# Ending of a fused projection and stream-mixing kernel re-ordered by tile, and its first loads put on one queue

## The reference, cut to what matters

```
h = einsum('bsi,boi->bso', x, weight[ids])          # 8 batches, 512 x 2048 by 2048 x 2048
hn = h * rsqrt(mean(h*h) + eps)
res, pre, post = hn@W_res.T+b, hn@W_pre.T+b, hn@W_post.T+b     # 16, 4 and 4 logits a token
H_res = (1-g)*I + g*sinkhorn(res, 50 iterations, tau 0.1)
pre, post = softmax(pre), softmax(post)
streams = h.reshape(B, T, 4, 512)
y = einsum('btnc,btn->btc', streams, pre) @ W_branch
out = x + einsum('btij,btjc->btic', H_res, streams) + einsum('btc,btn->btnc', y, post)
```

## Time and profile before

| | |
|---|---|
| median of 3 runs | 1717.91 us (1715.99 to 1718.01) |
| the profiled execution's own time | 1717.58 us |
| its span | 1715.8 us |
| PE busy | 1686.2 us (98%) |
| DVE busy | 1425.7 us (83%) |
| ACT busy | 719.8 us (42%) |
| DMA | 252.41 MB, mean 147 GB/s |

### The profile page before, as it was taken

The page is one execution under the profiler, slowest core; times in us unless marked ns, Lnnn a source line. Parts: engine busy times, 40 slices in busy tenths (PEclk is TensorE's granted clock), DMA queues, the critical chain, the costliest instruction groups (busy, mean ns, idle before and its releaser), DMA issues.

```text
span 1715.8 us, 24502 instructions
## 1 busy us (share of the span) xinstructions
PE 1686.2 (98%) x7740; PEld 1363.0 (79%) x7740; DVE 1425.7 (83%) x5973; ACT 719.8 (42%) x1167; POOL 101.5 (6%) x142
## 2 busy tenths in 40 slices
PE   8999999999999999999999999999999999999886
PEld 7888888888888878887888888888788887888773
DVE  4322499988998889988899979998899889998795
ACT  4433544244333343434433354424433454334563
POOL 0000000010000100000000000001000110001021
PEclk9999999999999999999999999999999999999999
DMA  6223423375233832358325562337522693238779
GB/s 238 87 92 125 152 87 111 99 216 189 99 109 113 253 140 98 103 151 264 99 90 128 186 212 98 111 102 218 187 96 87 168 317 101 89 97 217 175 136 247
DMA packets 68865, 252.41 MB, mean 147 GB/s; under 512 B 7936, under 2 KB 8064, under 8 KB 67840
## 3 DMA queue, kind: packets, MB, share of 16 engines
q1 hardware_dynamic: 48576, 177.97, 31.6%
q0 software_dynamic: 19584, 71.31, 17.5%
q10 hardware_dynamic: 576, 1.57, 0.3%
HBM read 203.63 MB, written 42.99 MB: 144 GB/s over the span
## 4 chain that ended last, share of the span: by engine, by line
PE 89%; issue 4%; DMA 3%; DVE 3%; POOL 1%; ACT 1%; SPq 0%; DVEq 0%; POOLq 0%; ACTq 0%
PE acc L1169 77%; PE y_ps L1247 3%; PE turn_ps L1205 3%; PE logit_ps L1213 2%; PE logit_ps L1216 2%; DVE piece L1027 2%; DMA x_raw<-xn 1%; DMA piece<-xn 1%; DMA out<-late_own 1%; DVE w_lo L778 1%; PE acc L1356 1%; PE y_ps L1237 1%; POOL out L427 1%; PE acc L1194 0%; PE turn_ps L1225 0%
## 5 line engine op out<-in xcount | busy, mean ns | idle before, releaser
L1169 PE MATMUL acc<-w_hi,x_hi 128*128 128x512 f32 x2040 | 807.7, 396 | 0.0
L1169 PE MATMUL acc<-w_hi,x_lo 128*128 128x512 f32 x2040 | 796.0, 390 | 0.0
L1169 PE MATMUL acc<-w_lo,x_hi 128*128 128x512 f32 x2040 | 794.4, 389 | 0.0
L473 ACT ACTIVATE w_hi<-w_raw 128x1024 fp32r<-128x1024 f32 x255 | 269.3, 1058 | 441.6 <-DMA w_raw<-wt 441.5
L1169 PEld LDWEIGHTS acc<-w_hi,x_lo 128*128 128x128 f32 x2040 | 382.9, 188 | 82.3
L1169 PEld LDWEIGHTS acc<-w_hi,x_hi 128*128 128x128 f32 x2040 | 383.2, 188 | 79.6
L1169 PEld LDWEIGHTS acc<-w_lo,x_hi 128*128 128x128 f32 x2040 | 383.6, 188 | 76.7
L778 DVE TENSOR_TENSOR w_lo<-w_raw,w_hi 128x1024 fp32r<-128x1024 f32 x256 | 311.7, 1218 | 133.8 <-ACT w_hi L473 122.4
L1027 DVE SCALAR_TENSOR_TENSOR piece<-cond,kern,piece 128x512 f32<-128x512 f32 x416 | 283.1, 746 | 5.0 <-DMA piece<-xn 5.0
L963 DVE RECIPROCAL vec<-vec 128x8 f32<-128x8 f32 x1536 | 240.4, 198 | 0.0
L961 DVE TENSOR_REDUCE vec<-work 128x8 f32<-128x32 f32 x1536 | 238.0, 194 | 0.2
(11 more groups left out here) (161 smaller groups left out, 835.7 us busy)
## 6 DMA issues: line engine op xcount, KB each, us to landing
w_raw<-wt SPq DMA_DIRECT2D x255, 512.0 KB, 3.5
out<-piece POOLq DMA_DIRECT2D x62, 512.0 KB, 5.4
x_raw<-xt SPq DMA_DIRECT2D x61, 512.0 KB, 5.4
piece<-xn POOLq DMA_DIRECT2D x56, 512.0 KB, 7.1
out<-late_own POOLq DMA_DIRECT2D x10, 512.0 KB, 9.0
grouped<-cond SPq DMA_DIRECT2D x16, 256.0 KB, 9.4
x_raw<-xn POOLq DMA_DIRECT2D x8, 512.0 KB, 12.0
out<-x_raw SPq DMA_DIRECT2D x7, 512.0 KB, 10.9
```

The costliest lines, as they stand in the source:

```text
L473: nc.scalar.activation(w_hi[:, unit % HI_SLOTS, :, :], w_raw[:, unit % LO_SLOTS, :, :], ACT.Copy).then_inc(w_hi_ready, 1)
L1169: mm = nc.tensor.matmul(acc[t][:], stationary, moving, start=(chunk == 0 and m == 0), stop=(chunk == CHUNKS - 1 and m == 2))
```

## The change

- SP issues the loads of x units 0, 1 and 2, which ACT issued; unit 0 goes ahead of the load of the adapter's number. Units 0 and 1 of batch 0 are done by kind of product (`unit_by_product`), and 32 warm-up transposes are issued, not 24.
- `spread_pre(t)` writes the identity times pre (4 x 128x128), and `weigh_and_turn(t)` multiplies the unweighed streams by it, in the place of `weigh_streams` and `turn_terms`.
- Late rows have 11 slots, not 5: six lie in the free half of `cond`. Late tiles are split in two buffers alternately (cond_t, xpre_t), the own tiles in a third (end_t). Late products rotate over three banks of `acc`; the fourth is `sum_bank`.
- Planes 0 to 9 are summed in `sum_bank` one by one between the other work and copied as before. Planes 10 to 15 are summed late and stay in six banks (`keep_base`); the mixing product adds onto them. Their residual comes by three plain loads on SP (`load_last_residual`), so POOL has five residual adds, not eight. The mixing runs in `MIX_ORDER` (10 to 15, then 0 to 9) over all eight banks.
- The order of `ending()` on PE and ACT, and of POOL's transfers, is written out anew.

```diff
-LATE_OWN, LATE_SLOTS = 3, 5
+LATE_OWN, LATE_SLOTS = 3, 11
+COPIED = 10
+MIX_ORDER = tuple(range(COPIED, 16)) + tuple(range(COPIED))
+BLOCK_ORDER = (2, 3, 0, 1)
...
-WARM_UP = 24
-SUMS_AFTER = 2
+BY_PRODUCT = 2
+WARM_UP = 32
...
-        end_c, end_term = cond[:, 1, :, :, :], cond[:, 0, :, :, :]
+        end_c = cond[:, 1, :, :, :]
+        pre_diag = cond[:, 0, 0, :, :].rearrange("p t (j m) -> p t j m", j=STREAMS)
...
+        for j in range(1, STREAMS):
+            late_out += [cond[:, 0, j, 2 * h:2 * h + 2, :] for h in range(2)]
         late_out += [piece[:, i, :, :] for i in range(OUT_SLOTS // 2, OUT_SLOTS)]
+        end_t = nc.alloc_sbuf_tensor_at("end_t", [P, 2, C], F32R, offset=xpre_place)
+        late_parts = (cond_t, xpre_t)
...
-        end_bank = acc + y_ps
+        end_bank = (turn_ps, acc[3], acc[0], acc[1], acc[2], y_ps[0], y_ps[1], logit_ps)
+        sum_bank = acc[TILES - 1]
...
+            def load_last_residual(q):
+
+                wait_unit(sp, BATCHES - 1, 3 * PASS_UNITS + q)
+                sp.dma_start(end_out[:, 2 * q:2 * q + 2, :], xn[(BATCHES - 1) * MIX_PAIRS + q, :, :]
+                             .rearrange("p (e c) -> p e c", e=2)).then_inc(x_in[q], 16)
...
-                for q in range(MIX_PAIRS - 1):
-                    store_planes(2 * q, 2)
-                for e in range(2):
-                    store_planes(END_PLANES - 2 + e, 1)
+                for n in MIX_ORDER[0:END_PLANES - 2:2]:
+                    store_planes(n, 2)
+                for n in MIX_ORDER[END_PLANES - 2:]:
+                    store_planes(n, 1)
...
-                adapter = adapter_of(b)
                 if not end:
+                    for k in range(UNIT_CHUNKS):
+                        sp.dma_start(x_raw[:, k, :], xt[0, :, k * TOKENS:(k + 1) * TOKENS]
+                                     ).then_inc((x_first_in, x_in[0])[k], 16)
+                    adapter = adapter_of(b)
                     for k in range(UNIT_CHUNKS):
                         sp.dma_start(w_raw[:, 0, k, :],
                                      wt[bass.ds(index(adapter * UNITS), 1), :,
                                         k * C:(k + 1) * C].rearrange("a p c -> (a p) c")
                                      ).then_inc((w_first_in, w_in[0])[k], 16)
                     for u in range(1, PASS_UNITS):
-                        if u >= FIRST_X:
...
+                    if last and U - 3 * PASS_UNITS - 1 in range(COPIED // 2, MIX_PAIRS):
+                        load_last_residual(U - 3 * PASS_UNITS - 1)
...
-            for r in range(LATES * MIX_PAIRS):
-                add_late(r)
-            for q in range(MIX_PAIRS):
-                add_end(q)
+            def add_late_tile(k):
+                add_late(2 * k)
+                add_late(2 * k + 1)
+
+            for k in range(4):
+                add_late_tile(k)
+            add_end(0)
+            add_end(1)
+            add_late_tile(4)
+            add_end(2)
+            add_late_tile(5)
+            add_late_tile(6)
+            add_end(3)
+            add_end(4)
+            add_late_tile(7)
...
-            for k in range(UNIT_CHUNKS):
-                act.dma_start(x_raw[:, k, :], xt[0, :, k * TOKENS:(k + 1) * TOKENS]
-                              ).then_inc((x_first_in, x_in[0])[k], 16)
-            for u in range(1, FIRST_X):
-                act.dma_start(x_raw[:, 2 * u:2 * u + 2, :],
-                              xt[u, :, :].rearrange("p (k s) -> p k s", k=UNIT_CHUNKS)
-                              ).then_inc(x_in[u], 16)
...
-                        weigh(end_term[:, j, t, :], end_c[:, j, t, :],
-                              logit[:, t, NRES + j:NRES + j + 1], pre_weighed)
+                        weigh(pre_diag[:, t, j, :], ident[:],
+                              logit[:, t, NRES + j:NRES + j + 1], pre_spread)
...
-                    if k == 0:
+                    if k < 2:
                         act.wait_ge(project_done, job + C // P)
                     else:
-                        act.wait_ge(late_y_ready, k)
-                    nc.scalar.activation(cond_t[:, 0, :], late_turn[k][:], ACT.Copy
+                        act.wait_ge(late_y_ready, k - 1)
+                    nc.scalar.activation(late_parts[k % 2][:, 0, :], late_turn[k][:], ACT.Copy
...
-
                 act.wait_ge(mixed, 1 + c * MIX_PAIRS)
-                weigh_streams(0)
+                spread_pre(0)
+                late_low(1)
+                spread_pre(1)
...
+                spread_late(3)
+                copy_base(2)
+                late_low(4)
+                pre_high(2)
+                answer_log_step(asks, 1)
+                copy_base(3)
+                pre_low(2)
+                copy_base(4)
+                spread_late(4)
+                late_high(5)
...
+                late_high(7)
+                copy_base(8)
+                copy_y(3)
+                late_low(7)
+                copy_base(9)
+                spread_late(7)
...
+                        bank = end_bank[MIX_ORDER.index(n) % len(end_bank)]
+                        if n < COPIED:
+                            dve.wait_ge(end_added[n // 2], 16)
+                        else:
+                            dve.wait_ge(x_in[n // 2], (BATCHES + 1) * 16)
+                        dve.wait_ge(block_mixed, MIX_ORDER.index(n) + 1)
+                        tt(end_out[:, n, :], bank[:], end_out[:, n, :],
                            ALU.add).then_inc(out_ready, 1)
...
-                    block_of(0)
-                    for t in range(TILES):
-                        if t + 1 < TILES:
-                            block_of(t + 1)
-                        for g in range(GROUPS):
-                            add_base(t * GROUPS + g)
+                    block_of(BLOCK_ORDER[0])
+                    block_of(BLOCK_ORDER[1])
+                    for place, n in enumerate(MIX_ORDER):
+                        if place == 2:
+                            block_of(BLOCK_ORDER[2])
+                        if place == 6:
+                            block_of(BLOCK_ORDER[3])
+                        add_base(n)
...
+            def unit_by_product(u):
 
                 for m in range(3):
                     for k in range(UNIT_CHUNKS):
-                        if m == 0 and k == 0:
+                        if m == 0 and k == 0 and u == 0:
                             pe.wait_ge(first_hi_ready, 2)
-                        if m == 0 and k == 1:
-                            pe.wait_ge(x_hi_ready, 1)
-                            pe.wait_ge(w_hi_ready, 1)
+                        elif m == 0:
+                            pe.wait_ge(x_hi_ready, u + 1)
+                            pe.wait_ge(w_hi_ready, u + 1)
...
+                def weigh_and_turn(t):
+
+                    pe.wait_ge(pre_spread, (t + 1) * STREAMS)
...
-                            mm = nc.tensor.matmul(y_ps[t % 2][:, cols], end_term[:, j, t, cols],
-                                                  ident[:], start=(k == 0 and j == 0),
+                            mm = nc.tensor.matmul(y_ps[t % 2][:, cols], end_c[:, j, t, cols],
+                                                  pre_diag[:, t, j, :], start=(k == 0 and j == 0),
...
-                    if k >= TILES:
-                        pe.wait_ge(late_spread, (k - TILES + 1) * STREAMS)
-                    multiply(cond_t, acc[k % TILES]).then_inc(late_y_ready, 1)
+                    if k > 2:
+                        pe.wait_ge(late_spread, (k - 2) * STREAMS)
+                    multiply(late_parts[k % 2], acc[k % 3]).then_inc(late_y_ready, 1)
...
                 def sum_base(n):
 
-                    t, bank = n // GROUPS, n % len(end_bank)
-                    pe.wait_ge(y_block_ready, (t + 1) * STREAMS)
-                    if n == 0:
+                    if n > 0:
+                        pe.wait_ge(base_ready, n)
+                    y_product(n, sum_bank).then_inc(base_summed, 1)
+
+                def keep_base(n):
+
+                    bank = end_bank[MIX_ORDER.index(n)]
+                    if bank is turn_ps:
+                        pe.wait_ge(late_lo_ready, LATE_TILES - 1)
+                    elif bank is sum_bank:
+                        pe.wait_ge(base_ready, COPIED)
+                    elif bank is acc[2]:
+                        pe.wait_ge(late_spread, (LATE_TILES - 2) * STREAMS)
+                    elif bank is acc[0]:
+                        pe.wait_ge(late_spread, (LATE_TILES - 1) * STREAMS)
+                    elif bank is acc[1]:
                         pe.wait_ge(late_spread, LATE_TILES * STREAMS)
-                    if n >= len(end_bank):
-                        pe.wait_ge(base_ready, n - len(end_bank) + 1)
-                    nc.tensor.matmul(end_bank[bank][:], y_block[:, t, n % GROUPS, :],
-                                     y_sb[:, t, :], start=True, stop=True
-                                     ).then_inc(base_summed, 1)
+                    y_product(n, bank)
```

(56 more changed lines are left out.)

149 lines of the change are left out of this document (81 added, 68 removed).

## The result

Over six runs the changed kernel takes **1707.03 us** at the median (1705.93 to 1709.62) against 1717.99 for the kernel before (six runs, 1715.99 to 1718.88): ratio 0.9939, 95% interval 0.9926 to 0.9952. The forecast was 1705.0 with a range of 1702.5 to 1710.

The account below looks back on a forecast made before the run. TensorE's unbroken chain was taken to bound the middle, leaving only the two ends to gain: 1717.58 - 3.6 (start) - 9.1 (tail) = 1704.9 for the profiled execution; stated as 1705.0, range 1702.5 to 1710.

Parts of the forecast that it names:

- Start: Kernel start: weights land earlier, first product at 8.1 us, clock at 2.4 GHz, first unit shorter; together 3.6 us gained.
- Rival B: Start: weights land no earlier and the clock falls as before; 0.8 us lost instead of 3.6 gained, 1709.3; chance 0.08.
- A microsecond saved before 20 us comes off the end: Middle, 20 to 1598 us: TensorE's chain is unbroken, with 1.8 us of waits, so the start's gain reaches the end.
- Order: Ending: reordered work on TensorE and ScalarE lets the matrix's spread start at 1684.0 instead of 1687.70, 3.7 us earlier.
- rival D: Ending: ScalarE answers VectorE's question at 1644.90 late, delaying its chain; a 3 us slip gives 1708; chance 0.04.
- Mixing: Ending: mixing starts at 1686.8, runs at 0.86 us a plane, and is through its last add at 1701.6.
- rival A: Mixing: short TensorE waits around the spread bring 1.2 GHz, costing 1.6 to 1.8 us, so 1706.7; chance 0.22.
- each of the two is shorter than that one: Argument against a slow mixing clock: waits of 1.6 and 1.9 us are shorter than the 2.31 that lowered it.
- End: Residuals and stores: no add waits for a residual, DMA queue empty at 1688.3, end at 1706.7; tail 9.1 us less.
- rival C: Ending: DMA still busy at 1688 with late rows, stores fall behind, end 3 to 5 us later; chance 0.12.
- The last store: Kernel end: the last store was to take 5.1 us to the end, kept from the kernel before.
- Rival E: The end is bound elsewhere, and only the start or nothing comes through: 1714 to 1718; chance 0.04.

Follow-up runs that it names:

- new_start_alone: The kernel before with only the new start; 1715.53 us, ratio 0.9984.
- the twins: Changed kernel without residual reads of batches 0 to 6, once with the new start (1703.19 us), once with the old (1705.99 us).
- old_start: Changed kernel with the start of the kernel before (loads, 24 warm-up transposes, only unit 0 by product); 1709.89 us, ratio 0.9947.
- nores_old: Changed kernel with the old start and without the residual reads of batches 0 to 6; 1705.99 us, ratio 0.9924.
- copy_first: Changed kernel with ScalarE copying the fourth y product before answering VectorE's second question, not behind it; 1706.86 us, ratio 0.9929.
- change_again: The changed kernel as it is, run again on the chip of the follow-up runs; 1705.98 us, ratio 0.9922.
- late_warm: Changed kernel with 74 warm-up transposes instead of 32; 1708.68 us, ratio 0.9938.
- w_first: Changed kernel with SyncE, late in each batch, waiting for weights to land before asking for the next batch's x; 1717.78 us, ratio 0.9994.
- slots5: Changed kernel with 5 slots for late rows instead of 11; 1706.70 us, ratio 0.9924.
- copied16: Changed kernel with all 16 y products copied, none kept in PSUM, no residuals read ahead, mixing order 0 to 15; 1715.80 us, ratio 0.9975.
- fill12: Changed kernel with 12 dummy transposes on TensorE between the matrix's spread and the mixing; 1705.03 us, ratio 0.9920.
- w_first_fill: w_first with 12 dummy transposes added between the matrix's spread and the mixing; 1718.04 us, ratio 0.9993.

## Why the prediction was right, and where it was not

*Start.* First weight issued at 4.47 (forecast 4.30), landed after 2.45 us (3.1), product at 7.63 (8.1), clock 1.00: 3.95 us against 3.6. Rival B is out. Whether the weights landed sooner because less was ahead of them or because of the queue, no run separates.

*"A microsecond saved before 20 us comes off the end."* This step failed in the profiled execution, where all 3.94 us were lost by batch 7. In the times it holds in part: 2.8 us in new_start_alone, 2.8 between the twins, 1.4 and 4.3 for old_start against the change's two ratios (0.9947 - 0.9939 and 0.9947 - 0.9922, times 1719). The term was 3.6, and about 2.8 is what the runs give. Two things were missed. TensorE's 1.8 us of waits in one profile said that this execution had little waiting, not that the middle could not wait: VectorE waits for residual reads, the way from there to TensorE has only 1.0 us to spare, and the kernels with these reads lose 1.1 to 5.1 us in the middle. And the profiled start of before was on the late side: its first gather was at 218.0, in old_start at 217.8 and in nores_old at 216.5.

*Order.* Branch_late(0) was forecast at 1607.7 (1607.83), weigh_and_turn(2) to end at 1642.3 (1641.41), TensorE to wait 2.8 us (3.45), the spread at 1684.0 (1683.72). ScalarE was in time for VectorE's question by 2.84 us (1.9), so VectorE's chain did not move, and rival D is out. That TensorE's speed doesn't count here and the matrix does is shown by copy_first. So the hit at 1684.0 says little for the prices of TensorE's waits: it was ready 0.21 us ahead of the matrix here and 1.87 us ahead in change_again, and the spread began with the matrix both times.

*Mixing.* Forecast to start at 1686.8 (1686.67) and to run at 0.86 us a plane: it did from the fourth add on, and rival A, priced at 1.6 to 1.8 us, came true with 0.80 + 0.84 = 1.64 us for two adds. It was given 0.22, and a mixing slower than 0.86 a plane stood among the signs of being wrong. The step that failed is the argument "each of the two is shorter than that one": with 0.21 us of wait ahead of the spread and 1.84 behind it the clock fell.

*End.* The last add ended at 1703.13 (forecast 1701.6, rival A's 1.64 being the difference), without a wait for a residual. The DMA engines were free at 1688, as forecast: their share is 0.06 from 1688 to 1691, so rival C is out. The last store was mis-sized: 5.1 us were kept from before, 2.8 it took. The 5.1 had been paid with the engines at a share of 1.03, and the sum itself had them free when the stores begin, so the price should have been that of a queue in which only these stores stand. Rival E is out by old_start, whose ending alone gives 9.1 us. So the ending gave 27.0 - 19.5 = 7.5 plus 2.3 = 9.8 us where 9.1 were said.

For the profiled execution the sum was 1704.9, and it took 1707.7: 3.6 us of the start that did not arrive, 1.5 more to the end of the last add, 2.3 less for the last store. That the total came this close is in part luck, because the errors had both signs. Of the mechanisms the order of the ending, the residuals and the free DMA engines were right; the clock in the mixing, the middle and the last store were not.

## What to carry to other kernels

A chain without waits in one profile proves only that execution: before carrying a gain at the start through to the end, look at the waits of the engines that feed the chain, where a late transfer shows while it is still absorbed (here VectorE's 0.6 to 1.5 us for residuals), and take marks from several profiles. When a wait is moved instead of removed, count the clock as well: an idle time of 1.84 us of TensorE right ahead of the last, serial part cost another 1.6 us in the clock, and twelve dummy transposes in it took that away. Take the price of a last store from transfers that find the queue as it will be then.

## What the runs showed of the hardware

Ten profiles have the new ending without the dummy transposes, and in all ten some of the mixing's first planes ran at half the clock. In six (change, old_start, late_warm, both twins, w_first) TensorE had waited at most 0.25 us for the matrix and spread it at full clock; the granted clock fell at the end of the 1.84 us wait ahead of the mixing or within 1.2 us behind it. In the other four it had fallen before that wait: in change_again and slots5 during the spread, behind a wait of 1.87 and 1.86 us, in copy_first within the wait of 5.57 us, and in copied16 behind one of 2.14. In fill12 and w_first_fill, with 0.53 us of the wait left, it stayed at 1.00. In copied16 it then stayed at half through three single products with waits of 0.69 us ahead of each. But a wait of 3.45 us at 1645 us did not always bring it down: in the change and in fill12 the granted clock over 1648 to 1657 us was 0.81 and 0.83, in change_again, behind the same wait, 1.00:

```profile
1648.00:1657.00 9.00, 9.00 (x62) 8.06 (x63) 8.83 (x75) 4.31 (x8) 2.63 (x3) 1.00 0.89 143
```

And 512 KB of weights, issued from 1360 to 1400 us, landed after 3.7 and 4.1 us at the median in the twins, with the DMA engines 0.74 and 0.71 busy, and after 5.8 to 7.6 us in the ten kernels with the reads, at 0.93 to 0.95; the 5.8 is old_start's, the 7.6 the change's.
